# One VectorE product of 2,048 elements instead of two of 1,024 in a state-space scan kernel

## The reference

```python
def step(h, inp):
    xt, dtt, Bt, Ct = inp
    dA = jnp.exp(dtt[:, :, None] * A)
    h = dA * h + (dtt * xt)[:, :, None] * Bt[:, None, :]
    y = jnp.einsum('ben,bn->be', h, Ct)
    return (h, y)
```

## Time and profile before

| | |
|---|---|
| Median of 3 runs | 12675.65 us (12661.51 to 12689.12) |
| Profiled execution | 12639.29 us, its span 12637.5 us |
| Products at L1257 | 2048, 2389.7 us busy |
| Scans at L1268 | 4096, 9093.4 us busy |
| TensorE clock granted, mean | 0.901 of full speed |

### The profile page before, as it was taken

The page is one execution under the profiler, slowest core; times in us unless marked ns, Lnnn a source line. Parts: engine busy times, 40 slices in busy tenths (PEclk is TensorE's granted clock), DMA queues, the critical chain, the costliest instruction groups (busy, mean ns, idle before and its releaser), DMA issues.

```text
span 12637.5 us, 179504 instructions
## 1 busy us (share of the span) xinstructions
PE 10215.3 (81%) x51484; PEld 5829.8 (46%) x51484; DVE 11838.3 (94%) x7032; ACT 10856.0 (86%) x23460; POOL 11415.9 (90%) x5972
## 2 busy tenths in 40 slices
PE   5678878888787887878878888887878878788887
PEld 2334544445444444544445444454544445444445
DVE  5999999999999999999999999999999999999992
ACT  5888988898888998988989888898889989888882
POOL 4999999999999999999999999999999999999992
PEclk7778989999898998989989898998989989889898
DMA  2223333333333333333333333333333333333332
GB/s 85 84 86 115 123 111 129 124 109 115 115 129 116 118 126 105 131 114 123 122 115 116 113 127 123 109 123 108 130 113 120 123 112 129 111 126 123 108 111 97
DMA packets 610252, 1458.92 MB, mean 115 GB/s; under 512 B 68928, under 2 KB 110032, under 8 KB 604672
## 3 DMA queue, kind: packets, MB, share of 16 engines
q1 hardware_dynamic: 609152, 1446.18, 35.2%
HBM read 1355.09 MB, written 90.83 MB: 114 GB/s over the span
## 4 chain that ended last, share of the span: by engine, by line
issue 27%; PE 21%; ACT 17%; POOL 16%; DVE 15%; DMA 1%; DVEq 0%; POOLq 0%; SPq 0%; ACTq 0%
POOL state L1298 13%; DVE state L1268 10%; ACT state L1082 6%; ACT v_sb L1095 5%; PE driven L882 5%; PE q_ps L837 4%; DVE driven L1257 3%; PE y_ps L904 3%; PE q_ps L824 2%; PE p_ps L745 1%; PE p_ps L753 1%; POOL v_sb L1376 1%; PE b_ps L872 1%; ACT L1082 1%; PE p_ps L769 1%
## 5 line engine op out<-in xcount | busy, mean ns | idle before, releaser
L1298 POOL TENSOR_TENSOR state<-state,c_rep 128x1024 f32<-128x1024 f32 x4096 | 9660.7, 2390 | 773.3 <-DVE state L1268 767.6
L1268 DVE TENSOR_TENSOR_SCAN state<-state,driven 128x1024 f32<-128x1024 f32 x4096 | 9093.4, 2269 | 260.7 <-PE driven L882 252.0
L1082 ACT ACTIVATE state<-ud_rep,cols_sb 128x512 f32<-128x512 f32 x8192 | 5212.3, 710 | 6.6 <-PE y_ps L904 4.1
L1095 ACT ACTIVATE v_sb<-u_t,b_t 128x128 f32<-128x128 f32 x12288 | 4062.3, 505 | 940.0 <-PE driven L882 936.6
L882 PE MATMUL driven<-consts_sb,v_sb 128*128 128x128 f32 x16384 | 2631.8, 313 | 1284.8 <-DVE state L1268 1260.5
L882 PEld LDWEIGHTS driven<-consts_sb,v_sb 128*128 128x128 f32 x16384 | 2130.5, 161 | 2445.0 <-DVE state L1268 1745.6
L904 PE MATMUL y_ps<-state,consts_sb 128*32 128x512 f32 x16384 | 2420.8, 668 | 568.8 <-POOL state L1298 567.9
L1257 DVE TENSOR_TENSOR driven<-ud_rep,b_ps 128x1024 f32<-128x1024 f32 x2048 | 2389.7, 1212 | 18.1 <-DMA ud_rep<-ud_rows 18.1
L837 PE MATMUL q_ps<-hid,wq_sb 128*128 128x256 f32 x7936 | 2049.5, 403 | 144.7 <-ACT hid L1060 76.0
L837 PEld LDWEIGHTS q_ps<-hid,wq_sb 128*128 128x128 f32 x7936 | 1478.9, 196 | 1012.9 <-issue 821.4
L1376 POOL TENSOR_TENSOR v_sb<-u_t,b_t 128x512 f32<-128x512 f32 x1024 | 1070.3, 1045 | 36.5 <-issue 23.6
(11 more groups left out here) (141 smaller groups left out, 5533.5 us busy)
## 6 DMA issues: line engine op xcount, KB each, us to landing
c_rep<-bc_rows SPq DMA_DIRECT2D x2048, 256.0 KB, 3.0
ud_rep<-ud_rows SPq DMA_DIRECT2D x512, 512.0 KB, 4.2
wq_sb<-in_h SPq DMA_DIRECT2D x512, 512.0 KB, 3.9
wq_sb<-in_f SPq DMA_DIRECT2D x128, 512.0 KB, 4.0
wp_sb<-in_win SPq DMA_DIRECT2D x64, 512.0 KB, 4.5
dt_sb<-conv_taps SPq DMA_DIRECT2D x32, 1024.0 KB, 5.5
ud_rows<-u_pad SPq DMA_DIRECT2D x128, 256.0 KB, 3.3
ud_rows<-dt_sb SPq DMA_DIRECT2D x128, 256.0 KB, 3.5
```

What stands on the lines that cost most here:

```text
L1082: ins = act.activation(state[:, unit % STATE_RING, j, :], ud_rep[:, nth % 2, j, 1, :], ACT.Exp, scale=a_neg[:, d, c, j, g:g + 1])
L1095: ins = act.activation(v_sb[:, unit // 2 % V_RING, tt, :, :, n].rearrange("p j e -> p (j e)"), u_t[:, nth % 2, tt, :], ACT.Identity, scale ...
L1268: dve.tensor_tensor_scan(flat, flat, driven[:, q % DRIVE_RING].rearrange("p j t -> p (j t)"), 0.0, ALU.mult, ALU.add).then_inc(scanned, 1)
L1298: pool.tensor_tensor(part, part, c_rep[:, unit % ROW_RING, :].unsqueeze(1).to_broadcast([P, 2, T]), ALU.mult).then_inc(was_read, 1)
```

## The change

VectorE makes the drive of an even unit in one product over all four rows and all four banks of `driven`. The product waits for the unit's predecessor to be scanned in full (`2 * unit` half units), both scans of the even unit wait for the one product, and `dve_driven` counts one for each even unit instead of two. TensorE's wait in `spread` is renumbered and means the same as before.

```diff
-        def dve_drives(at, unit, h):
+        def dve_drives(at, unit):
 
-            return of_body(at, 2 * len(DVE_UNITS), 2 * (unit // 2) + h + 1) + 1
+            return of_body(at, len(DVE_UNITS), unit // 2 + 1) + 1
...
-                pe.wait_ge(dve_driven, dve_drives(at, unit, 0) - 1)
+                pe.wait_ge(dve_driven, dve_drives(at, unit) - 1)
...
-            def drive(at, unit, h):
+            def drive(at, unit):
                 nth = unit % UNITS // NG
-                if h == 0:
-                    if unit % NG == 0:
-                        dve.wait_ge(ud_in[nth % 2], pass_loaded(at, unit // NG))
-                    dve.wait_ge(b_spread, of_body(at, len(DVE_UNITS), unit // 2 + 1))
-                dve.wait_ge(scanned, of_body(at, HALVES, 2 * unit + h - DRIVE_RING + 1) + DRIVE_RING)
-                dve.tensor_tensor(driven[:, h], u_rows(unit)[:, 2 * h:2 * h + 2],
-                                  b_ps[:].unsqueeze(1).to_broadcast([P, 2, T]), ALU.mult).then_inc(dve_driven, 1)
+                if unit % NG == 0:
+                    dve.wait_ge(ud_in[nth % 2], pass_loaded(at, unit // NG))
+                dve.wait_ge(b_spread, of_body(at, len(DVE_UNITS), unit // 2 + 1))
+                dve.wait_ge(scanned, of_body(at, HALVES, 2 * unit) + DRIVE_RING)
+                dve.tensor_tensor(driven[:].rearrange("p r i t -> p (r i) t"), u_rows(unit),
+                                  b_ps[:].unsqueeze(1).to_broadcast([P, JC, T]), ALU.mult).then_inc(dve_driven, 1)
...
                 if unit in DVE_UNITS:
-                    dve.wait_ge(dve_driven, dve_drives(at, unit, h))
+                    dve.wait_ge(dve_driven, dve_drives(at, unit))
...
                 if at.kind == "first":
-                    drive(at, 0, 0)
-                    drive(at, 0, 1)
+                    drive(at, 0)
...
-                            drive(at, unit + 1, 0)
-                            drive(at, unit + 1, 1)
+                            drive(at, unit + 1)
```

## The result

The changed kernel takes 12800.43 us (median of 5 runs, 12796.78 to 12816.68) against 12665.64 for the kernel before in the same runs: a ratio of 1.0116, 95% interval 1.0104 to 1.0129. It is slower by some 147 us by the ratio, 135 by the medians. The profiled execution has a span of 12814.3 us against 12637.5, 177 us more; it is one of the slower executions of this kernel, the one of before was one of the faster.

A forecast was written before the change was run, and what follows sets the result against it. VectorE was taken to bound the kernel: 215 us for newly exposed waits, less 16, 52 and 15 us covered or absorbed, gave +132 us on the median 12676, so 12808 us; 8-in-10 range 12735 to 12915.

The forecast's parts named there:

- The bound: VectorE, busy 94% of the span, sets the pace; whatever is added between its instructions is added to the end time.
- clean cycle: Undisturbed VectorE time from one even unit's products to the next, with four scans: 10.97 us before, 11.18 foretold after.
- The price of each gap: Last odd scan to product, +0.12 us; product to even unit's first scan, +0.09; together 0.21 a pair, 215 us.
- some 0.12 us: Claimed cost on VectorE of waiting for one's own predecessor: 0.08 us of lost overlap and 0.04 of wait.
- What takes some of it off: Deductions from the 215 us: 16 for side instructions, 52 for transpose waits, 15 for waits before side steps such as y_ps.
- covered second gaps: In 135 pairs a side instruction stands between product and scan and hides the exposed wait: 16 us less.
- the waits in front of an odd unit's first scan: 250 VectorE waits for TensorE's transposes, said to absorb at most 0.21 us each, 52 us in all.
- those in front of the second: 160 VectorE waits for transposes before an odd unit's second scan, said to move with a late scan and absorb nothing.
- it would be faster, as one instruction fewer: Rival: waits for the predecessor cost nothing on VectorE, 0.03 us gained a pair, 31 us less, 12645; chance 0.08.
- No change: Rival: the other engines absorb nearly all of the 0.21 us a pair, time 12676; chance 0.05.
- Much slower: Rival: the long product meets the disturbance that lengthens L1240, 2090 us on top, 14900; chance 0.01.
- TensorE's clock: TensorE's clock changes level within the execution and could move either time by some tens of us.

The follow-up runs named there:

- second gap, wait alone: Kernel before, two products: even unit's first scan waits for the second product right ahead, its other wait on a small semaphore instruction; 12713.29 us, ratio 1.0049.
- first gap: Kernel before, two products: only the first product's wait changed, to the last odd scan right ahead of it; 12753.19 us, ratio 1.0087.
- second gap: Kernel before, two products: only the even unit's first scan changed, to wait for the second product right ahead; 12777.84 us, ratio 1.0107.
- changed kernel, wait alone: Changed kernel with a small semaphore instruction taking the wait for spread or decays, so product and scan carry the predecessor's wait; 12792.54 us, ratio 1.0105.
- both gaps, waits alone: Kernel before, two products: first product and even unit's first scan wait for their predecessors, other waits on small semaphore instructions; 12791.11 us, ratio 1.0115.
- both gaps: Kernel before, two products: first product waits for the last odd scan, even unit's first scan for the second product; 12878.02 us, ratio 1.0189.
- three waits: Kernel before, two products: first product, second product and even unit's first scan each wait for the instruction right ahead; 12931.29 us, ratio 1.0226.

## Why the prediction was right, point by point

**The bound.** VectorE's order of instructions was the place to read. The clean cycle was foretold as 11.18 us (11.16 to 11.20) and is 11.18 in the loop, which holds 14 of the 16 batches; in the two straight-line ones it is 11.32 to 11.33, outside the range given.

**The price of each gap.** +0.12 for the first, +0.09 for the second: both are what the changed kernel shows in the loop. Product duration 2.29 foretold, 2.295 to 2.297 measured in all 1024. What fell short is "some 0.12 us" as one price for all such waits. It is 0.12 to 0.14 where the instruction carries the wait for its predecessor itself, and about 0.07 more where that wait stands on a semaphore instruction in front of it. In the straight-line bodies that made +0.35 to +0.36 a cycle instead of +0.21: 128 cycles by 0.15, 19 us that the sum lacked. The setup copies, from which the 0.04 was taken, carry the wait themselves.

**What takes some of it off.** The clean price is 896 x 0.21 + 128 x 0.36 = 234 us; less the 16 us of covered second gaps, 218. Summed from start to start over both traces, the products and scans themselves take 211 us more. The time rose by 147, so 64 to 71 us were absorbed; 67 were foretold. The total is right, its make-up is not, so that the total fits is partly luck. In the two profiled executions, which lie 177 us apart, only 34 to 41 were absorbed.

The step said that the waits in front of an odd unit's first scan shrink by 52 us and those in front of the second stay. Counted over the timeline, the first kind went from 251 waits (184.5 us) to 185 (179.0), the second from 160 (67.5) to 122 (51.9): 21 us together, and three quarters of it where nothing was to be absorbed. The prediction named this as the sign of being wrong about the size: waits for transposes that shrink by much less than 50 us. That a wait of the first kind takes up 0.21 us each time is not what happened: 66 of these waits went, and the rest grew longer in the mean, from 0.74 to 0.97 us.

The other items between the profiled executions, which the sum had not or had as 15 us in all: y_ps waits 23 us less, waits of L1238 9 less, waits of L1244 6 less, waits of scans with no releaser in the profile 5 less, L1244 25 us less busy, against 33 us of new waits for ScalarE's decays, 8 us more in L1238, and 12 us more in the network's sums (L1228). With the 21 these sum to -37, so 211 - 37 = 174 against 177 measured. The items are read off; what moved each of them was not tried, and this case has such shifts in both directions.

How much of a given clean price reaches the time can be read from all kernels, each price being 896 times the cycle's rise in the loop and 128 times that in the straight-line bodies:

| kernel | clean cycle, loop / straight | price, us | measured by the ratio, us | share |
|---|---|---|---|---|
| second gap, wait alone | 11.10 / 11.11 | 134 | 62 | 0.46 |
| first gap | 11.11 / 11.19 | 154 | 110 | 0.71 |
| second gap | 11.17 / 11.17 | 205 | 135 | 0.66 |
| changed kernel, wait alone | 11.18 / 11.18 | 215 | 133 | 0.62 |
| changed kernel | 11.18 / 11.33 | 234 | 147 | 0.63 |
| both gaps, waits alone | 11.25 / 11.25 | 287 | 145 | 0.51 |
| both gaps | 11.32 / 11.39 | 367 | 239 | 0.65 |
| three waits | 11.45 / 11.52 | 500 | 286 | 0.57 |

The share lies between 0.46 and 0.71, without a trend in the price. The prediction's 132 / 215 = 0.61 is in the middle of it. What sets a kernel's place in that band was not found; the reordering of TensorE's work moved the changed kernel by 70 us with the clean cycle unchanged, so such shifts of the side work are large enough to make it. With that order in both kernels the same price of 234 us made only 43 us (12728.26 less 12685.17), a share of 0.18: a forecast of the time from the clean cycle holds for one arrangement of the other engines.

**The rivals.** That it would be faster, as one instruction fewer: without the exposed waits merging could be worth the 0.03 of the prediction or the 0.07 measured with them, but no kernel here has the long product without them. It needs all four banks free, so it cannot start before the last odd scan has ended; giving it other banks was not tried. The page "VectorE: DVE Perf Modes" of the Trainium skill says under "The DRAIN you can't avoid" that "the semaphore costs nothing extra here", measured there on eight copies in a row; the runs here show 0.12 to 0.20 us for each semaphore wait on the instruction right ahead, with the same instructions otherwise. No change: 252 us of waits for the transposes did not take up the price. Much slower: the product's 2295 to 2297 ns show nothing of what lengthens L1240 to 4332 ns in the median.

**TensorE's clock.** The granted clock was 0.901 in the mean before and 0.887 after. It is lower in all the slower kernels (0.886 with three waits). The prediction allowed some tens of us for it without saying which way. Behind the last product, where the change has next to no part, VectorE's waits for the network's sums (L1228) went from 219.4 to 225.5 us. Whether the clock makes part of the lost time or only goes along with it was not separated.

## What to carry to other kernels

Count how many instructions back on the same engine each wait's producer stands. An instruction that waits for one two back can start while the one right ahead still finishes; one that waits for its direct predecessor can't, and here that costs 0.12 to 0.20 us each time, against 0.07 us that one instruction fewer brings (0.03 by the prediction's estimate where the gaps are hidden). Look also at where the built program puts that wait: on the instruction itself it costs 0.07 us less than on one of its own in front. Merging two operations of a ring halves its depth, so ask first which waits it moves from two back to one back.

## What the runs showed of the hardware that was not expected

A wait for the predecessor costs more where it stands on a semaphore instruction of its own: the gap between the predecessor's end and the start is 0.035 us where the waiting instruction carries the wait itself (changed kernel in the loop) and 0.103 to 0.105 where it carries another wait and the one for the predecessor stands in front of it (second-gap kernel, straight-line bodies). Of the longer gap 0.04 us lie before the semaphore instruction's start and 0.065 behind it. Putting the other wait on a semaphore instruction, so that the predecessor's moves onto the instruction, brings the clean cycle from 11.33 to 11.18 and from 11.32 to 11.25. Such an instruction costs nothing where its wait is met while something else still runs: the even scans of the kernel before have one too, in the cycle of 10.97. Swapping the two waits in the source was not tried.

The prices add up: 0.14 and 0.20 alone, 0.35 together, and 0.13 for a third. And an edit of TensorE's order that costs 0.23% in one kernel gains 0.57% in the other, whose only difference is VectorE's gaps.
